# A graph layer and its experts: the 38 lightest nodes as fourth step, the last steps full, scatters bounded and eight gathers later

## The chip, the cores and the metric

The kernel runs on one core of a Trainium2 chip. The metric is the device time of one execution in microseconds (us). The engines are called PE (TensorE), DVE (VectorE), ACT (ScalarE), POOL (GpSimd) and SP (SyncE).

## What is computed

A graph attention layer over 3,750 nodes with 256 features and 123,750 edges, and behind it a mixture of eight experts on every node, both with a residual. Cut to what matters:

```python
feat_all = jnp.einsum('ni,rhid->rnhd', layernorm(x), conv_weights)   # 8 relations, 4 heads of 64
e = leaky_relu(sum(feat_src * attn_l) + sum(feat_dst * attn_r))      # per edge and head
alpha = segment_softmax(e, edge_dst)
x = x + segment_sum(alpha[..., None] * feat_src, edge_dst) + h_bias
xf = layernorm(x)
cw = the two largest of softmax(xf @ gate_w + gate_b), per node
x = x + sum over e of cw[:, e] * (gelu(xf @ W1[e] + b1[e]) @ W2[e] + b2[e])
```

## The kernel before

**Phase 1** (up to about 258 us) works out the row `feat_all` of every (node, relation) and stores it in a table in DRAM, 264 floats a row. Beside it the nodes are ranked by their number of edges (the degree), heaviest first, and each node's row of x goes with its number, the start of its edges, its degree and its norm to `ranked`, where 128 nodes of like degree stand together. 3,750 nodes make 30 groups of 128; the last has only 38 nodes (`LAST`). I call the groups q0 (heaviest) to q29 (the 38 lightest). The other 90 rows of that group are filled from the tile `zeros`.

**Phase 2** works through 30 *windows* w = 0 to 29, one group each (`W` = 30). The line that makes `rank_f` in phase 1 says which group is which window: before, group q goes to window 2q in the first half, and to 57 - 2q in the second, so that heavy and light alternate: q0, q28, q1, q27, ... q14 last but one, and q29, which would be at -1, goes to the end. For a window:

- POOL issues one indirect gather per slot (L907): slot k brings the table row of edge k of each of the 128 nodes. 20 slots always, further ones while k is below the largest degree of the window, up to 40; a window with a larger degree gets its further slots (`xrows`) by 4 or 8 behind the gathers of the next window. A memset behind each second gather (L940) spaces them, and a tiny one (`space_end`, L973) ends a window. `rows` has two buffers, given back in four parts by DVE (`freed`).
- DVE adds the gathered scores (L1043), takes the exponents (with ACT), weighs the rows and adds them up; more than 32 slots take a branch of their own (`weighted(32, 40)` and three adds). I call a window with more than 32 slots heavy, any other light. `post` makes xo (L1173) and its norm z (L1184).
- The experts of window w run on PE (L1497 first product `hid`, L1511 second product `y`) and ACT (gelu, L1389) while DVE and ACT weigh window w + 1; DVE mixes y into xo (L1228, L1236), pair by pair of experts, and writes the row ids `oid` (L1242) to say that xo is ready.
- POOL scatters xo to the output (L915, `scatter`). Inside the gathers of window w it issues the scatter of window w - 3; it waits there for `out_ok`. Its queue is in order, so the gathers behind stand as well. The last three scatters come behind all gathers. DVE's L1173 waits for the scatter of two windows before (`out_done`).

Windows 0 and 1 are written out, the other 28 are a loop of 14 turns with two windows each. Behind the loop come the experts of the last window alone, with `LAST` = 38 nodes: `experts(u, LAST)`, `gelu(u, e, LAST)`, `mix(u, 1, p, st, LAST)`.

Of the kernel before, what the change touches and what calls it, by code (L numbers as in the profile page):

```python
# [20 lines left out]
ALU = mybir.AluOpType  # L21
ACT = mybir.ActivationFunctionType
F32 = mybir.dt.float32
I32 = mybir.dt.int32
# [5 lines left out]
P = 128  # L30
SLOTS = 8
# [133 lines left out]
def phase1(nc, sb, sem, env):  # L165
# [4 lines left out]
    N, D, E, R, H, HD, KD, HC, AGG, ROW, TN, T, J, EJ, W, NF, GN, NBINS, LAST, XW = (env[k] for k in (  # L170
        "N", "D", "E", "R", "H", "HD", "KD", "HC", "AGG", "ROW", "TN", "T", "J", "EJ", "W", "NF", "GN", "NBINS",
        "LAST", "XW"))
# [18 lines left out]
    with ctx:  # L191
# [16 lines left out]
        tmpT = t("tmpT", [TN, T])  # L208
# [29 lines left out]
        rank_f = t("rank_f", [TN, J])  # L238
# [3 lines left out]
        zeros = t("zeros", [P - LAST, XW])  # L242
# [58 lines left out]
        @block.sync  # L301
        def _(sp):
            def load_x(g):
                lo, hi = GROUPS[g]
                for a, b in parts:
                    sp.dma_start(x_all[a:b, lo:hi, 0:D], x_v[a:b, lo:hi, :]).then_inc(x_in[g], 16)

            load_x(0)
            for a, b in parts:
                sp.dma_start(dst_sb[a:b, :], dst_v[a:b, :]).then_inc(dst_in, 16)  # L310
            sp.dma_start(attnb[:, 0, :], attn_l.rearrange("r h d -> (r h d)").partition_broadcast(P)).then_inc(attn_in[0], 16)
            load_x(1)
            sp.dma_start(attnb[:, 1, :], attn_r.rearrange("r h d -> (r h d)").partition_broadcast(P)).then_inc(attn_in[1], 16)
            for a, b in parts:
                sp.dma_start(src_sb[a:b, :], src_v[a:b, :]).then_inc(et_in, 16)
                sp.dma_start(typ_sb[a:b, :], typ_v[a:b, :]).then_inc(et_in, 16)
            load_x(2)
            load_x(3)
            sp.wait_ge(pool_const, 2)
            sp.dma_start(ranked_v[LAST:P, W - 1, :], zeros[:]).then_inc(zero_out, 16)  # L320

            sp.wait_ge(erow_ok, 1)
            for a, b in parts:
                sp.dma_start(edge_row[0:E].rearrange("(p e) -> p e", p=TN)[a:b, :], erow[a:b, :]).then_inc(erow_out, 16)
            sp.dma_start(edge_row[E:GN].rearrange("(p e) -> p e", p=1), zero_u[:]).then_inc(erow_out, 16)

            sp.wait_ge(ranked_out, 16 * J)
            for i, (lo, hi) in enumerate(RANKED):
                sp.dma_start(rank_sb[:, lo:hi, :], ranked_v.bitcast(I32)[:, lo:hi, D:D + 4],
                             allow_slow_non_contiguous=True).then_inc(rank_in[i], 16)  # L330

            for i in range(NSTG):
                sp.wait_ge(stored[i], NP * len(range(i, T, NSTG)))

        @block.gpsimd
        def _(pool):
            g = nc.gpsimd
            g.memset(ident[:], 0.0).then_inc(ident0, 1)
            g.memset(lower[:], 1.0).then_inc(ident0, 1)
            pool.wait_ge(ident0, 2)  # L340
            g.affine_select(out=ident[:], in_=ident[:], compare_op=ALU.not_equal, fill=1.0, base=0,
                            pattern=[[-1, P]], channel_multiplier=1).then_inc(ident_ok, 1)
            g.affine_select(out=lower[:], in_=lower[:], compare_op=ALU.is_ge, fill=0.0, base=-1,
                            pattern=[[1, TN]], channel_multiplier=-1).then_inc(pool_mask, 1)
            g.memset(zero_u[:], 0).then_inc(pool_const, 1)
            g.memset(zeros[:], 0).then_inc(pool_const, 1)
            g.iota(node_i[:], pattern=[[1, J1]], base=0, channel_multiplier=J).then_inc(pool_const, 1)
            g.iota(bin_i[:], pattern=[[1, NBINS]], base=-BIN, channel_multiplier=0).then_inc(pool_const, 1)
            g.iota(slot_i[:], pattern=[[1, CHUNK]], base=0, channel_multiplier=0).then_inc(pool_const, 1)
            for i in range(NSTG):  # L350
                for h in range(H):
                    g.memset(stage[i][:, :, h * HC + HD:h * HC + HD + 1], 1.0).then_inc(cols_ok, 1)

            for j in range(J1):
                if j in (0, JD):
                    pool.wait_ge(chunk_ok, 1 if j == 0 else 2)
                g.indirect_dma_start(dchunk[:, j, :], None, dst.rearrange("(c e) -> c e", e=SEARCH),  # L357
                                     bass.IndirectOffsetOnAxis(chunk_u[:, j:j + 1], 0)
                                     ).then_inc(chunk_in[landing_of(j)], 16)

            pool.wait_ge(rank_ok, 1)
            pool.wait_ge(zero_out, 16)
            for j in range(J):
                g.indirect_dma_start(ranked, bass.IndirectOffsetOnAxis(rank_u[:, j:j + 1], 0), x_all[:, j, :],  # L364
                                     None).then_inc(ranked_out, 16)

            pool.wait_ge(erow_out, NP + 16)
            for w in range(W):
                if w in starts_at:
                    pool.wait_ge(rank_in[starts_at[w]], 16)  # L370
                g.indirect_dma_start(idx_all[:, w, :], None, edge_row.rearrange("(n o) -> n o", o=1),
                                     bass.IndirectOffsetOnAxis(rank_sb[:, w, 1:2].bitcast(U32), 0)
                                     ).then_inc(idx_in, 16)
                g.memset(spacer[:, w, :], 0)
            pool.wait_ge(idx_in, 16 * W)

        @block.vector
        def _(dve):
            v = nc.vector
            st = Steps(dve, dstep)  # L380

            def go(ins):
                st.did(ins)
                st.wait()

            v.memset(ones[:], 1.0).then_inc(ones_ok, 1)
            dve.wait_ge(pool_const, 5)
            st.did(v.tensor_copy(bin_f[:], bin_i[:]))
            st.did(v.tensor_copy(slot_id[:], slot_i[:]))
            go(v.tensor_copy(node_f[:], node_i[:]))  # L390
# [90 lines left out]
            go(v.tensor_scalar(rank_p[:], rank_i[:], P - 1, None, ALU.bitwise_and))  # L481
            go(v.tensor_scalar(rank_i[:], rank_i[:], 7, None, ALU.logical_shift_right))
            go(v.tensor_copy(rank_f[:], rank_i[:]))
            go(v.tensor_scalar(tmpT[:], rank_f[:], -2.0, 2.0 * W - 3.0, ALU.mult, ALU.add))
            go(v.scalar_tensor_tensor(out=rank_f[:], in0=rank_f[:], scalar=2.0, in1=tmpT[:], op0=ALU.mult, op1=ALU.min))
            go(v.tensor_scalar(tmpT[:], rank_f[:], 0.0, float(W), ALU.is_lt, ALU.mult))
            go(v.tensor_tensor(rank_f[:], rank_f[:], tmpT[:], ALU.add))
            v.scalar_tensor_tensor(out=rank_u[:], in0=rank_p[:], scalar=float(W), in1=rank_f[:], op0=ALU.mult,  # L488
                                   op1=ALU.add).then_inc(rank_ok, 1)
# [150 lines left out]
def phase2(nc, sb, sem, env):  # L640
# [258 lines left out]
    def _(pool):  # L899
# [8 lines left out]
                                     bass.IndirectOffsetOnAxis(idx[:, col + k:col + k + 1], 0)  # L908
                                     ).then_inc(landed, 16)

        def scatter(v, par, n=P):

            pool.wait_ge(out_ok, v + 1)
            alone(pool, pool_passed)
            q.indirect_dma_start(out, bass.IndirectOffsetOnAxis(oid[par][0:n, :], 0), xo[par][0:n, :],  # L915
                                 None).then_inc(out_done[par], 16)

        def static_rows(w, par, half):

# [28 lines left out]
            for k in range(SURE):  # L948
                if k == 2 * EDGE and (not isinstance(w, int) or w >= 1):
                    fills(w * 3)  # L950
                if k == SLOTS and (not isinstance(w, int) or w >= 3):
                    scatter(w - 3, 1 - par)
                if k % SLOTS == 0:
                    freed_by(k // SLOTS)
                last = spaced_gather(k)
                if k in (SURE // 2 - 1, SURE - 1):
                    last.then_inc(spaced, 1)
# [48 lines left out]
        windows(pool, window)  # L1006
        scatter(W - 3, 1)
        scatter(W - 2, 0)
        scatter(W - 1, 1, LAST)
        for i in range(2):  # L1010
            pool.wait_ge(out_done[i], 16 * (W // 2))

# [1 line left out]
    def _(dve):  # L1014
# [216 lines left out]
        def mix(u, par, p, st, n=P):  # L1231

            dve.wait_ge(w2_ok, u * NE + 2 * p + 2)
            for e in (2 * p, 2 * p + 1):
                st.wait()
                st.did(v.scalar_tensor_tensor(out=xo[par][0:n], in0=y_ps[p % 2][0:n, (e % 2) * D:(e % 2 + 1) * D],  # L1236
                                              scalar=cw[0:n, e:e + 1], in1=xo[par][0:n], op0=ALU.mult, op1=ALU.add))
# [82 lines left out]
        u = W - 1  # L1320
        st = mix_start(u, 1)
        for p in range(PAIRS):
            mix(u, 1, p, st, LAST)
        finish(u, 1, st)

    @block.scalar
    def _(act):
# [57 lines left out]
        def gelu(u, e, n=P):  # L1385
            act.wait_ge(hid_ok, u * NE + e + 1)
            after(act, w2_ok, u * NE + e - 1)
            for m in range(KH):
                last = a.activation(hT[e % 2][:, m, 0:n], hid_ps[e % 2][:, m * P:m * P + n], ACT.Gelu,  # L1389
                                    bias=b1t[:, e, m:m + 1])  # L1390
            last.then_inc(gelu_ok, 1)
# [63 lines left out]
        z_in(u)  # L1455
        gate_den(u)
        for e in range(NE):
            gelu(u, e, LAST)
            if e == 1:
                cwt_in(u)  # L1460

    @block.tensor
    def _(pe):
# [92 lines left out]
        windows(pe, window)  # L1556
        u = W - 1
        z_turn(u)
        experts(u, LAST)


_INS = ['x', 'src', 'dst', 'edge_type_8', 'L0_gnn_conv_weights', 'L0_gnn_attn_l', 'L0_gnn_attn_r', 'L0_gnn_h_bias',
# [23 lines left out]
```

## Time and profile before

| | |
|---|---|
| median of 3 runs | 1844.96 us (1844.57 to 1847.32) |
| the profiled execution: its time, its span | 1841.54 us, 1839.5 us |
| busy: PE, DVE, ACT, POOL | 1291.8, 1294.8, 778.6, 1334.4 us |
| gathers into `rows`, into `xrows` | 982, 24 |
| first and last gather of window 0 to 29 | 258.21 us to 1737.74 us |
| last scatter starts | 1828.68 us |

Gathers of each window, counted on POOL between its end markers (the degree of the group's heaviest node, at most 40):

| windows | before |
|---|---|
| 0 to 9 | 40, 24, 40, 25, 40, 26, 40, 27, 39, 28 |
| 10 to 19 | 38, 28, 38, 29, 37, 30, 36, 30, 36, 31 |
| 20 to 29 | 35, 31, 35, 32, 34, 32, 34, 33, 33, 21 |

Window 0 has 16 extra slots, windows 2 and 4 have 4 each. Windows 27 and 28 are the groups q15 and q14, window 25 is q16 with 32 slots. The span goes from the first to the last instruction; an engine's busy time says nothing of whether the others wait for it.

### The profile page before, as it was taken

How to read it: one execution, taken by the hardware profiler on the slowest of the kernel's cores; microseconds unless marked ns; L12 is line 12 of the kernel's file. 1: busy time of each engine (PE TensorE's matmuls, PEld its weight loads, DVE VectorE, ACT ScalarE, POOL GpSimd, SP SyncE). 2: the span in 40 equal slices, each digit the busy share in tenths (PEclk: the TensorE clock that was granted, in tenths of full speed). 3: DMA queues.
4: the chain of work that ended last, by engine and by line, in shares of the span. 5: the costliest groups of instructions: out<-in, count | busy, mean ns of one | idle time of the engine just before them, and what ended most of it. 6: DMA issues, size and time to landing. Idle time of an engine off the chain costs nothing.

```text
span 1839.5 us, 28715 instructions
## 1 busy us (share of the span) xinstructions
PE 1291.8 (70%) x6881; PEld 1040.7 (57%) x6881; DVE 1294.8 (70%) x2578; ACT 778.6 (42%) x2829; POOL 1334.4 (73%) x1702
## 2 busy tenths in 40 slices
PE   6999940037684777677767677777777685867787
PEld 2444420026574666666666566667666575756675
DVE  7660032668887888787878787878787878878881
ACT  3544410225354444444444444444444444544441
POOL 0727748688788788888888888888888888888600
PEclk9999975568797888888888888888879797888887
DMA  8758576333333333333333333333333333333300
GB/s 227 228 160 216 162 212 210 82 93 100 83 100 94 89 99 100 101 98 101 99 99 101 100 98 101 98 101 101 100 99 99 98 100 101 99 99 101 81 4 4
DMA packets 86819, 204.06 MB, mean 111 GB/s; under 512 B 32475, under 2 KB 44693, under 8 KB 82371
## 3 DMA queue, kind: packets, MB, share of 16 engines
q0 software_dynamic: 57552, 147.97, 29.8%
q10 hardware_dynamic: 9596, 33.95, 6.1%
q1 hardware_dynamic: 19485, 20.52, 4.0%
q14 instruction: 174, 1.43, 0.3%
q8 instruction: 12, 0.20, 0.0%
HBM read 162.22 MB, written 40.07 MB: 110 GB/s over the span
## 4 chain that ended last, share of the span: by engine, by line
POOL 41%; issue 18%; DVE 12%; PE 5%; DVEq 3%; POOLq 3%; ACT 2%; DMA 1%; ACTq 0%; SPq 0%
POOL rows L907 31%; POOL space_ring L940 7%; DVE fold_ps L1084 3%; PE y_ps L1511 2%; PE hid_ps L1497 2%; DVEq L67 2%; DVE rows L1080 1%; DVE xo L1236 1%; ACT rows L1400 1%; POOL out_dram L915 1%; POOL space_edge L940 1%; POOL xrows L907 1%; POOLq L920 1%; POOLq L964 1%; POOLq L979 1%
## 5 line engine op out<-in xcount | busy, mean ns | idle before, releaser
L907 POOL DMA_INDIRECT rows<-table,idx_st x982 | 943.5, 961 | 253.1 <-issue 243.8
L1511 PE MATMUL y_ps<-w,hT 128*128 128x256 f32 (+1 forms) x1920 | 508.3, 421 | 258.7 <-ACT hT L1389 258.7
L1511 PEld LDWEIGHTS y_ps<-w,hT 128*128 128x128 f32 (+1 forms) x1920 | 385.9, 208 | 345.8 <-ACT hT L1389 282.9
L1497 PE MATMUL hid_ps<-zT,w 128*128 128x128 f32 (+1 forms) x3840 | 497.3, 293 | 0.0
L1497 PEld LDWEIGHTS hid_ps<-zT,w 128*128 128x128 f32 x3840 | 485.9, 208 | 13.3 <-issue 10.8
L1400 ACT ACTIVATE rows<-rows,ex 128x65 f32<-128x65 f32 x1320 | 326.0, 346 | 114.0 <-DVE ex L1071 114.0
L1389 ACT ACTIVATE hT<-hid_ps,b1t 128x128 f32<-128x128 f32 (+1 forms) x960 | 269.6, 363 | 209.9 <-PE hid_ps L1497 208.5
L1084 DVE TENSOR_TENSOR fold_ps<-rows,fold_ps 128x780 f32<-128x780 f32 (+1 forms) x348 | 326.9, 939 | 34.1 <-issue 4.7
L598 PE MATMUL feat_ps<-wc,xnT 128*125 128x512 f32 x480 | 220.7, 604 | 0.5 <-ACT xnT L533 0.5
L1080 DVE TENSOR_TENSOR rows<-rows,fold_ps 128x2340 f32<-128x2340 f32 (+1 forms) x76 | 189.7, 2529 | 3.3 <-issue 3.3
L940 POOL MEMSET space_ring<- 128x400 uint8 x414 | 187.3, 452 | 0.1
L1236 DVE SCALAR_TENSOR_TENSOR xo<-y_ps,cw,xo 128x256 f32<-128x256 f32 (+1 forms) x240 | 115.7, 482 | 37.6 <-PE y_ps L1511 31.3
L598 PEld LDWEIGHTS feat_ps<-wc,xnT 128*125 128x125 f32 x480 | 86.8, 190 | 91.1 <-issue 90.5
L1470 PE MATMUL zt_ps<-ident,z 128*128 128x128 f32 x60 | 16.9, 375 | 154.9 <-DVE z L1184 154.9
L546 ACT COPY stage<-feat_ps 125x512 f32<-125x512 f32 x120 | 69.5, 585 | 115.1 <-PE feat_ps L598 114.9
L915 POOL DMA_INDIRECT out_dram<-xo,oid x30 | 30.2, 1005 | 105.3 <-DVE oid L1242 101.0
L1470 PEld LDWEIGHTS zt_ps<-ident,z 128*128 128x128 f32 x60 | 8.6, 193 | 157.0 <-DVE z L1184 157.0
L1377 ACT COPY zT<-zt_ps 128x256 f32<-128x256 f32 x30 | 11.2, 372 | 180.1 <-PE zt_ps L1470 180.1
L1355 ACT ACTIVATE th<-e_diff 128x160 f32<-128x160 f32 x30 | 10.1, 336 | 173.9 <-DVE e_diff L1061 173.9
L357 POOL DMA_INDIRECT dchunk<-in_dst_dram,chunk_u x31 | 40.5, 1305 | 58.0 <-DVE chunk_u L436 48.8
L1481 PE MATMUL gate_ps<-ident,xnw 128*128 128x128 f32 x60 | 12.0, 284 | 78.7 <-ACT xnw L1366 78.7
L364 POOL DMA_INDIRECT ranked<-x_all,rank_u x30 | 35.7, 1190 | 41.0 <-DVE rank_u L488 32.1
(197 smaller groups left out, 1117.3 us busy)
## 6 DMA issues: line engine op xcount, KB each, us to landing
table<-stage ACTq DMA_DIRECT2D x30, 924.0 KB
rows<-table,idx_st POOLq DMA_INDIRECT x982, 2.8
w<-in_L_ffn_W_dram SPq DMA_DIRECT2D x16, 512.0 KB, 13.8
node_row<-ranked SPq DMA_DIRECT2D x30, 132.0 KB, 2.6
table<-stage ACTq DMA_DIRECT2D x30, 107.2 KB
x_all<-in_x_dram SPq DMA_DIRECT2D x2, 1120.0 KB
wc<-_L_gnn_conv_weights_dram ACTq DMA_DIRECT2D x2, 1024.0 KB, 8.0
attnb<-in_L_gnn_attn_l_dram SPq DMA_DIRECT2D x1, 1024.0 KB, 12.5
```

The lines of the kernel that those rows point to most:

```text
L546: a.copy(stage[i % NSTG][:, b * RB:(b + 1) * RB, 0:AGG].rearrange("p r (h c) -> p r h c", h=H)[:, :, :, 0:HD], feat_ps[b][0:TN, :].rearran ...
L598: last = m.matmul(feat_ps[b][0:TN, :], xnT[i % NXT][:, k, :], wc[:, k, b * BANK:(b + 1) * BANK], start=(k == 0), stop=(k == KD - 1))
L907: q.indirect_dma_start(buf[:, k, :], None, table, bass.IndirectOffsetOnAxis(idx[:, col + k:col + k + 1], 0)).then_inc(landed, 16)
L915: q.indirect_dma_start(out, bass.IndirectOffsetOnAxis(oid[par][0:n, :], 0), xo[par][0:n, :], None).then_inc(out_done[par], 16)
L940: return q.memset(spacing(k // 2), 0)
L1080: return v.tensor_tensor(o, r, bc(ex_ps[:, :, lo:hi].rearrange("p h k -> p k h"), 3, HC), ALU.mult)
L1084: return v.tensor_tensor(lanes[:, 0:n], rows[par][:, lo:lo + n, 0:AGG], lanes[:, 0:n], ALU.add)
L1236: st.did(v.scalar_tensor_tensor(out=xo[par][0:n], in0=y_ps[p % 2][0:n, (e % 2) * D:(e % 2 + 1) * D], scalar=cw[0:n, e:e + 1], in1=xo[par][ ...
L1389: last = a.activation(hT[e % 2][:, m, 0:n], hid_ps[e % 2][:, m * P:m * P + n], ACT.Gelu, bias=b1t[:, e, m:m + 1])
L1400: last = a.activation(r, r, ACT.Copy, scale=ex[:, h, k:k + 1])
L1497: last = t.matmul(hid_ps[e % 2][:, m * P:m * P + n], w1[:, e, k, m * P:(m + 1) * P], zT[:, k, 0:n], start=(k == 0), stop=(k == KD - 1))
L1511: last = t.matmul(y_ps[p % 2][0:n, (e % 2) * D:(e % 2 + 1) * D], hT[e % 2][:, k, 0:n], w2[:, e, k, :], start=(k == 0), stop=(k == KH - 1))
```

## The change

Four things:

1. *The order.* `rank_f` sends group q to window 2q up to q15, and to 61 - 2q from q16 on; q15, which would be at 30, goes to window 1. So the order is q0, q15, q1, q29, q2, q28, q3, q27, ... q14, q16. By the counts above, the gathers are then 40, 33, 40, 21, 40, 24, 40, 25, 39, 26 in windows 0 to 9; 38, 27, 38, 28, 37, 28, 36, 29, 36, 30 in 10 to 19; and 35, 30, 35, 31, 34, 31, 34, 32, 33, 32 in 20 to 29.
2. *The last window is full*: `LAST` goes out of the experts, gelus and mixes behind the loop.
3. *The filling rows* now lie in window 3 and carry the node number 3750 and more; all scatters have a bound, `bounds_check=N - 1`, and rows beyond it are skipped. POOL makes `zeros` with two memsets and an iota in place of one memset.
4. *A scatter's place*: behind gather 16 of a window instead of gather 8.

```diff
-            sp.wait_ge(pool_const, 2)
-            sp.dma_start(ranked_v[LAST:P, W - 1, :], zeros[:]).then_inc(zero_out, 16)
+            sp.wait_ge(pool_const, 4)
+            sp.dma_start(ranked_v[LAST:P, 3, :], zeros[:]).then_inc(zero_out, 16)
...
-            g.memset(zeros[:], 0).then_inc(pool_const, 1)
+            g.memset(zeros[:, 0:D], 0).then_inc(pool_const, 1)
+            g.memset(zeros[:, D + 1:XW], 0).then_inc(pool_const, 1)
+            g.iota(zeros[:].bitcast(I32)[:, D:D + 1], pattern=[[1, 1]], base=N, channel_multiplier=1).then_inc(pool_const, 1)
...
-            dve.wait_ge(pool_const, 5)
+            dve.wait_ge(pool_const, 7)
...
-            go(v.tensor_scalar(tmpT[:], rank_f[:], -2.0, 2.0 * W - 3.0, ALU.mult, ALU.add))
+            go(v.tensor_scalar(tmpT[:], rank_f[:], -2.0, 2.0 * W + 1.0, ALU.mult, ALU.add))
             go(v.scalar_tensor_tensor(out=rank_f[:], in0=rank_f[:], scalar=2.0, in1=tmpT[:], op0=ALU.mult, op1=ALU.min))
-            go(v.tensor_scalar(tmpT[:], rank_f[:], 0.0, float(W), ALU.is_lt, ALU.mult))
+            go(v.tensor_scalar(tmpT[:], rank_f[:], float(W), 1.0 - W, ALU.is_ge, ALU.mult))
...
-        def scatter(v, par, n=P):
+        def scatter(v, par):
 
             pool.wait_ge(out_ok, v + 1)
             alone(pool, pool_passed)
-            q.indirect_dma_start(out, bass.IndirectOffsetOnAxis(oid[par][0:n, :], 0), xo[par][0:n, :],
-                                 None).then_inc(out_done[par], 16)
+            q.indirect_dma_start(out, bass.IndirectOffsetOnAxis(oid[par][:], 0), xo[par][:], None,
+                                 bounds_check=N - 1, oob_is_err=False).then_inc(out_done[par], 16)
...
-                if k == SLOTS and (not isinstance(w, int) or w >= 3):
+                if k == 2 * SLOTS and (not isinstance(w, int) or w >= 3):
                     scatter(w - 3, 1 - par)
...
-        scatter(W - 1, 1, LAST)
+        scatter(W - 1, 1)
...
-            mix(u, 1, p, st, LAST)
+            mix(u, 1, p, st)
...
-            gelu(u, e, LAST)
+            gelu(u, e)
...
-        experts(u, LAST)
+        experts(u)
```

POOL's program inside the loop, at the scatter of window w - 3 within the gathers of window w (`rows<-table` are the gathers, `out_dram<-xo` the scatter). Before:

```order
L907 DMA rows<-table,idx_st 128x264 [waits spaced]
L907 DMA rows<-table,idx_st 128x264
L940 MEMSET space_ring 128x400
L907 DMA rows<-table,idx_st 128x264 x2
L940 MEMSET space_ring 128x400
L915 DMA out_dram<-xo,oid 3750x256 [waits out_ok]
L927 REGISTER_ALU
L907 DMA rows<-table,idx_st 128x264 [waits freed]
```

And now, in the changed kernel, whose lines are numbered two higher here:

```order
L929 REGISTER_ALU
L909 DMA rows<-table,idx_st 128x264 [waits freed]
L909 DMA rows<-table,idx_st 128x264
L942 MEMSET space_ring 128x400
L909 DMA rows<-table,idx_st 128x264 x2
L942 MEMSET space_ring 128x400
L909 DMA rows<-table,idx_st 128x264 x2
L942 MEMSET space_ring 128x400
L909 DMA rows<-table,idx_st 128x264 x2
L942 MEMSET space_ring 128x400
L917 DMA out_dram<-xo,oid 3750x256 [waits out_ok]
L929 REGISTER_ALU
```

The scatter has moved past the eight gathers 8 to 15 and their four memsets, and past one wait for a freed part of the buffer.

The end of ACT's program, the gelus of the last window's experts. Before:

```order
L1377 COPY zT<-zt_ps 128x256
L1381 ACTIVATE gth<-lg,nm 128x8
L1383 ACTIVATE gden<-gth 128x8
L1389 ACTIVATE hT<-hid_ps,b1t 128x38 x8
L1406 COPY cwT<-gate_ps 8x128
L1389 ACTIVATE hT<-hid_ps,b1t 128x38 x24
```

Now:

```order
L1379 COPY zT<-zt_ps 128x256
L1383 ACTIVATE gth<-lg,nm 128x8
L1385 ACTIVATE gden<-gth 128x8
L1391 ACTIVATE hT<-hid_ps,b1t 128x128 x8
L1408 COPY cwT<-gate_ps 8x128
L1391 ACTIVATE hT<-hid_ps,b1t 128x128 x24
```

The instructions and their order are the same; each works on 128 nodes where it worked on 38. The same goes for PE's first products (128x128 in place of 128x38) and DVE's mixes (128x256 in place of 38x256).

## Rows read from the trace of the kernel before

**Rows 1.** Page, part 4: the chain that ended last, by engine.
```profile
POOL 41%; issue 18%; DVE 12%; PE 5%; DVEq 3%; POOLq 3%; ACT 2%; DMA 1%; ACTq 0%; SPq 0%
```

**Rows 2.** Page, part 5: POOL's indirect transfers (count | busy us, mean ns | idle before).
```profile
L907 POOL DMA_INDIRECT rows<-table,idx_st x982 | 943.5, 961 | 253.1 <-issue 243.8
...
L915 POOL DMA_INDIRECT out_dram<-xo,oid x30 | 30.2, 1005 | 105.3 <-DVE oid L1242 101.0
...
L357 POOL DMA_INDIRECT dchunk<-in_dst_dram,chunk_u x31 | 40.5, 1305 | 58.0 <-DVE chunk_u L436 48.8
```

**Rows 3.** Table by stage, line L907: stage, its length, POOL busy (count), clock, DMA.
```profile
654.30:1707.10 1052.80, 692.62 (x726) 0.85 0.37 100
1707.10:1737.90 30.80, 19.96 (x21) 0.78 0.44 97
```

**Rows 4.** POOL in order of time: start, us, engine, line, operation, idle before.
```profile
499.00 1.01 POOL L915 DMA_INDIRECT out_dram<-xo,oid  x1 [6.61 <-DVE oid L1242]
...
607.65 1.01 POOL L915 DMA_INDIRECT out_dram<-xo,oid  x1 [5.55 <-DVE oid L1242]
...
1707.01 0.13 POOL L973 MEMSET space_end<- 128x1 uint8 x1
```

**Rows 5.** DVE in order of time, L1043 of windows 0 to 6, 27 to 29.
```profile
360.04 0.19 DVE L1043 TENSOR_TENSOR score<-score,xrows 128x32 f32<-128x32 f32 x1 [13.63 <-SPq L858]
...
405.27 0.33 DVE L1043 TENSOR_TENSOR score<-score,rows 128x160 f32<-128x160 f32 x1 [0.18 <-issue]
...
448.79 0.38 DVE L1043 TENSOR_TENSOR score<-score,rows 128x160 f32<-128x160 f32 x1 [0.17 <-issue]
...
506.51 0.32 DVE L1043 TENSOR_TENSOR score<-score,rows 128x160 f32<-128x160 f32 x1 [0.26 <-issue]
...
548.05 0.33 DVE L1043 TENSOR_TENSOR score<-score,rows 128x160 f32<-128x160 f32 x1 [0.26 <-issue]
...
590.43 0.19 DVE L1043 TENSOR_TENSOR score<-score,xrows 128x32 f32<-128x32 f32 x1 [5.99 <-SPq L858]
...
615.16 0.32 DVE L1043 TENSOR_TENSOR score<-score,rows 128x160 f32<-128x160 f32 x1 [0.26 <-issue]
...
656.70 0.33 DVE L1043 TENSOR_TENSOR score<-score,rows 128x160 f32<-128x160 f32 x1 [0.26 <-issue]
...
1663.09 0.33 DVE L1043 TENSOR_TENSOR score<-score,rows 128x160 f32<-128x160 f32 x1 [0.26 <-issue]
...
1709.83 0.33 DVE L1043 TENSOR_TENSOR score<-score,rows 128x160 f32<-128x160 f32 x1 [0.26 <-issue]
...
1759.57 0.33 DVE L1043 TENSOR_TENSOR score<-score,rows 128x160 f32<-128x160 f32 x1 [0.26 <-issue]
```

**Rows 6.** Who waited for whom, DVE, 657.1 to 1711: us, times, longest.
```profile
DVE xo L1228 <- issue: 38.0, 11, 3.8
DVE score L1043 <- SPq L858: 29.8, 10, 4.2
...
DVE xo L1236 <- PE y_ps L1511: 10.1, 10, 1.7
```

**Rows 7.** All engines in order of time, end of window 29 and behind it.
```profile
1783.24 3.73 PE L1497 MATMUL hid_ps<-zT,w 128*128 128x128 f32 x32
...
1785.23 1.14 ACT L1389 ACTIVATE hT<-hid_ps,b1t 128x128 f32<-128x128 f32 x4 [4.10 <-PE hid_ps L1497]
1785.47 0.48 DVE L1173 SCALAR_TENSOR_TENSOR xo<-z,valid,xres 128x256 f32<-128x256 f32 x1
...
1789.85 0.41 DVE L1184 TENSOR_SCALAR z<-xo,mv,rstd 128x256 f32<-128x256 f32 x1
...
1802.92 3.76 PE L1497 MATMUL hid_ps<-zT,w 128*128 128x38 f32 x32
...
1804.93 0.84 ACT L1389 ACTIVATE hT<-hid_ps,b1t 128x38 f32<-128x38 f32 x4 [6.49 <-PE hid_ps L1497]
```

**Rows 8.** DVE in order of time, its first use of x.
```profile
10.54 1.08 DVE L397 BATCH_NORM_STATS2 stats<-x_all 125x6 f32<-125x256 f32 x3 [6.91 <-DMA x_all<-in_x_dram]
```

## The prediction

> **What bounds the kernel now.** I read four views. First the chain of work that ended last [rows 1]: GpSimd (POOL) holds 41% of it and nearly all of that is the gather line L907 [rows 2]. Then who waited for whom, and POOL's order in time. In the long stretch from 654.3 to 1707.1 us POOL issues 726 gathers and 22 scatters [rows 3]. With 1.0 us and a 0.3 us gap for a scatter and 0.3 us for the end marker of a window, 22 x 1.6 = 35.2 us are not gathers, so one gather costs (1052.8 - 35.2) / 726 = 1.402 us with its gap and its share of the pacing memsets. POOL waits for nobody there; before it, it waits twice for a scatter whose row ids are late, 6.61 and 5.55 us [rows 4].
>
> Then DVE's row "score + rows" at L1043, the first instruction that needs all of a window's gathered rows; I call its start landed(w) [rows 5]. It reads 405.27 for w=1 and 1709.83 for w=28. In the same long stretch DVE waited for rows 29.8 us in 10 of 22 windows, each time in an even one [rows 6]. So POOL leads by little: one pair of windows takes 2 x 1052.8 / 22 = 95.7 us on POOL, and on DVE (1053.1 - 29.8 + 10 x 0.3) / 11 = 93.3 us. Two more things: an even window carries a pause of 38.0 / 11 = 3.5 us before L1228, where DVE's loop goes back to its start; and the end is not balanced. POOL issues only 21 gathers for the last window (30.8 us, [rows 3]) while DVE needs 49.74 us for window 28, so landed(29) = 1759.57 is set by DVE, some 19 us after the last gather could have landed.
>
> **The change, part by part.** *The order.* The same 30 windows with the same 982 gathers run, so POOL's total stays. What moves is who stands where: 33 gathers instead of 24 in w=1, 21 instead of 25 in w=3, and 32 instead of 21 in w=29. Follow both engines.
>
> w=1: nine more gathers stand ahead of the extra slots of window 0, for which DVE already waits 13.63 us [rows 5]. All of 9 x 1.402 = 12.6 us passes on: landed(1) = 417.9. Window 1 now has over 32 slots, so DVE runs its extra branch. Window 27, heavy and without the loop pause, takes 1709.83 - 1663.09 = 46.7 us; window 1 took 43.5 us light, and four to five us are the branch, so 47.5 us is taken between 46.7 and 48.7: landed(2) = 465.4.
>
> w=2 took 57.7 us and w=3 41.5 us, with no wait for rows: landed(4) = 564.6. w=4 took 67.1 us, of which 5.99 - 0.3 = 5.7 us are a wait for its extra slots [rows 5]. These now come early enough, because POOL has run past DVE: 61.4 us, landed(5) = 626.0. w=5 again 41.5: landed(6) = 667.5, against 656.70 before. So DVE is 10.8 us late there.
>
> POOL in the same stretch: the scatter of w-3 is issued behind gather 16 instead of 8, that is 8 x 1.402 = 11.2 us later. Alone this would swallow the waits of 6.61 and 5.55 us. But DVE is late by then. In the trace the scatter at 499.00 comes 50.2 us after landed(2), the one at 607.65 comes 59.6 us after landed(4), 53.9 us without the 5.7 us wait. So the first now goes out at 465.4 + 50.2 = 515.6, the second at 564.6 + 53.9 = 618.5. POOL is at the second after 1.3 us of scatter, 24 gathers (33.6), window 5 with 24 gathers (35.2), four extra slots (5.0) and 16 gathers (22.4): 613.1. The wait does not vanish, it is still some 5 us. From 618.5: 1.3 for the scatter and 24 gathers at 1.41, so POOL is through window 6 at 653.7, within 1 us of before.
>
> From there to the end of window 28 it has 712 gathers instead of 726: 712 x 1.402 + 35.2 = 1033.4, end 1687.1, and rows land 2.8 us later (1707.01 to 1709.83, [rows 4, 5]): 1689.9. DVE over the same 22 windows: 1053.1 less the waits, 26.8, less 3.1 because w=27 is light now (46.7 against 93.3 - 49.7 = 43.6), 1023.2: landed(28) = 1690.7. Both chains give nearly the same; since whichever is later counts at each window, I take 1691, 18.8 us before 1709.83. Then window 28 unchanged 49.74 and window 29, still light (32 slots), 30.28 us from landed(29) to z [rows 5, 7]. POOL's 32 gathers take 32 x 1.402 + 1.6 = 46.5 us and end at about 1734, landing before DVE comes at 1740.7. This is where the gain lies: the last 11 gathers hide under a DVE window that had covered an idle POOL.
>
> *The scatter's place for those behind it.* Behind it on POOL stand gathers 17 and on. DVE reuses xo two windows later and waits for the scatter. It would go out 22.4 + 1.3 us after a window's gathers end and lands 2.4 us later, some 23.3 us after landed(w); DVE asks for it at L1173, in the light window 29 25.9 us behind landed(29) [rows 5, 7]. It costs nothing; if that cover of 2.6 us were gone (DVE is late, which makes it larger), each us over it would count once per window.
>
> *The last window at full width.* Nothing is narrower any more: 128 columns instead of 38 in the first products and in the gelus. Rows at both widths stand side by side [rows 7]: 32 first-product records 3.76 us at 38 columns, 3.73 at 128; four gelus 0.84 against 1.14. PE goes through a pair of experts in hid then y, and the gelus hide under y except the first of a pair: 4 x 0.30 at most, 0.6 taken. The rule of the Trainium skill speaks against this: "TensorE: Matmul & The Clock Gate", step by step, says that throughput follows the number of moving columns. An estimate by that page: 128 records x 90 columns at 2.4 GHz = 4.8 us, which would make the sum 4.8 us worse. The rows disagree with it here, as the weight loads between the products set their pace.
>
> *The bound in the scatter.* No scatter of the trace has one. Below: nothing. Above: a doubling, 1.0 us each. The nearest rows are POOL's own indirect transfers, 961, 1005 and 1305 ns for three kinds [rows 2]; a spread of 0.34 us. I take 0, since the form alone moves the time by 44 ns between L907 and L915. The 90 skipped rows of w=3 save nothing, they are off the path.
>
> *Start.* Two more small POOL instructions near 2 us, and DVE and SP wait for them; DVE then stands 6.91 us waiting for x anyway [rows 8]. Nothing. The rank formulas have as many instructions as before.
>
> **Sum.** 1709.83 to 1691 is -18.8; +0.6 for the gelus: -18.2 us against the profiled execution's 1841.54 us (span 1839.5 and 2.0 around it), 1823.3. The median shown is 1844.96, 3.4 above that execution, so 1844.96 - 18.2 = 1826.8.
>
> **Rivals.**
> *A, DVE's windows get longer when their pauses go.* In the even windows DVE waited about 3 us, in which PE and ACT caught up with the feed-forward part. L1236 already waits for y_ps 10.1 us in 10 windows [rows 6]. If that becomes the rule, 0.9 us per pair over 11 pairs takes 10 us: 1837. Against it: window 28 began without any wait and took 49.74 us, as the others. 20%.
> *B, the bounded scatter is dear* (the other side). Each us of it counts in POOL's 22 scatters of the long stretch. At the spread of 0.34 us: 7.5 us, 1834. It decides from 18.2 / 22 = 0.83 us each; at a doubling 22 us and 1849, slower. The Trainium skill, "DMA: Bandwidth & Descriptors", SWDGE vs HWDGE, says that GpSimd computes these descriptors in software, so that a test per row would be plain work. For slower 6%, for a loss of part of the gain 6%.
> *C, the order helps nothing*: the late start (10.8 us at landed(6)) is made up only through DVE's 26.8 us of waits. If two thirds of these are no slack, because DVE would have met PE or ACT there instead, 18 us are lost: 1845. 5%, and 2% for worse.
> *D, more gain*: DVE's chain is shorter (w=1 at 46, no wait at 618), and POOL leads: the pair then still costs POOL 94 us, so no more than 5 us: 1822. 8%, of which half below 1821.
>
> **Numbers.** My forecast, 1822 to 1832: 53%. About 0.2%, 3.7 us, is what a measurement of this kernel can tell from no change. Faster by more than that: 53 + 17 (A) + 6 (B) + 8 (D) = 84%; within it: 3 (A) + 5 (C) = 8%; slower 6 + 2 = 8%. The range 1820 to 1839 leaves out most of C, the dear B and the tail of D.
>
> **What would show it.** POOL's gathers of w=1 end near 361 us; landed(1) at 418, landed(2) near 465; scatter waits of a few us in w=4 and w=6 at gather 16; DVE's waits for rows nearly gone up to w=20; landed(28) near 1691, landed(29) near 1741, z near 1771; then 50 us to the end. An L1238 wait that grows in every window shows A; scatters of over 1.3 us show B. I am wrong if landed(28) stays near 1705, or if the last products at 128 columns take over 4 us for 32.

## The result

The changed kernel takes 1820.9 us (median of 4 runs, 1820.09 to 1821.53) against 1846.14 us before (4 runs, 1844.57 to 1848.05): ratio 0.9863, 95% interval 0.9846 to 0.988, 25.2 us less. The forecast was 1826.8 us, 18.2 us less. In a second measurement the pair took 1819.45 and 1842.71 us. The profiled execution takes 1820.09 us with a span of 1818.0, 21.5 us less than the span of before. The profiled execution of before (1841.54 us) lies 4.6 us under the median of its kernel, that of the changed kernel 0.8 us under its own; the other 3.8 us are that.

Part 4 of the page, the chain that ended last, and of part 5 the gathers and scatters of POOL. The lines of the changed kernel are numbered two higher.

```profile
DVE 35%; POOL 14%; issue 11%; PE 11%; DVEq 9%; ACT 5%; POOLq 1%; DMA 0%; ACTq 0%; SPq 0%
...
L909 POOL DMA_INDIRECT rows<-table,idx_st x982 | 944.8, 962 | 247.3 <-issue 236.8
...
L917 POOL DMA_INDIRECT out_dram<-xo,oid x30 | 30.6, 1020 | 82.5 <-DVE oid L1244 78.0
```

Before, POOL held 41% of the chain [rows 1]. Now DVE holds 35% and POOL 14% in this execution. In the repeat of the same kernel, further down, it is the other way round, with 33% for POOL and 20% for DVE. So the two chains are about equally long now, as the forecast had them, and neither leads clearly. The gathers cost what they did, and a bounded scatter 1020 ns for 1005 [rows 2].

POOL in order of time (start, us, engine, line, operation, idle before): the marker behind window 1, the two scatters for which it still waits, the markers behind windows 6 and 28.

```profile
360.41 0.12 POOL L975 MEMSET space_end<- 128x1 uint8 x1
...
515.18 1.03 POOL L917 DMA_INDIRECT out_dram<-xo,oid  x1 [5.61 <-DVE oid L1244]
...
619.71 1.01 POOL L917 DMA_INDIRECT out_dram<-xo,oid  x1 [3.89 <-DVE oid L1244]
...
654.78 0.12 POOL L975 MEMSET space_end<- 128x1 uint8 x1
...
1690.04 0.12 POOL L975 MEMSET space_end<- 128x1 uint8 x1
```

DVE in order of time, landed(w) for w = 1, 2, 4, 5, 6, 28, 29, then z of window 29.

```profile
417.63 0.33 DVE L1045 TENSOR_TENSOR score<-score,rows 128x160 f32<-128x160 f32 x1 [0.18 <-issue]
...
465.17 0.33 DVE L1045 TENSOR_TENSOR score<-score,rows 128x160 f32<-128x160 f32 x1 [0.17 <-issue]
...
566.49 0.32 DVE L1045 TENSOR_TENSOR score<-score,rows 128x160 f32<-128x160 f32 x1 [0.25 <-issue]
...
627.24 0.32 DVE L1045 TENSOR_TENSOR score<-score,rows 128x160 f32<-128x160 f32 x1 [0.26 <-issue]
...
668.82 0.32 DVE L1045 TENSOR_TENSOR score<-score,rows 128x160 f32<-128x160 f32 x1 [0.26 <-issue]
...
1691.97 0.33 DVE L1045 TENSOR_TENSOR score<-score,rows 128x160 f32<-128x160 f32 x1 [0.85 <-SPq L860]
...
1742.17 0.33 DVE L1045 TENSOR_TENSOR score<-score,rows 128x160 f32<-128x160 f32 x1 [0.26 <-issue]
...
1773.17 0.41 DVE L1186 TENSOR_SCALAR z<-xo,mv,rstd 128x256 f32<-128x256 f32 x1
```

| | before | forecast | measured |
|---|---|---|---|
| landed(1) | 405.27 | 417.9 | 417.63 |
| landed(2) | 448.79 | 465.4 | 465.17 |
| scatters that POOL waits for | 499.00, 607.65 | 515.6, 618.5 | 515.18, 619.71 |
| landed(6) | 656.70 | 667.5 | 668.82 |
| POOL behind window 28 | 1707.01 | 1687.1 | 1690.04 |
| landed(28) | 1709.83 | 1691 | 1691.97 |
| landed(29) | 1759.57 | 1740.7 | 1742.17 |
| z of window 29 | 1789.85 | 1771 | 1773.17 |
| z to the last row ids | 37.69 | 38.3 | 33.07 |

Up to z the forecast is within 3 us in every line (the two largest misses are 2.9 us at POOL's marker behind window 28 and 2.2 us at z), and z came 16.7 us earlier than before. The last line is off by 5.2 us, with the sign wrong.

Who waited for whom, DVE, in 660 to 1692 us (us, times, longest), the stretch of [rows 6]:

```profile
DVE xo L1230 <- issue: 38.8, 11, 3.9
...
DVE xo L1238 <- PE y_ps L1513: 12.4, 14, 1.6
DVE score L1045 <- issue: 5.4, 21, 0.3
```

The 29.8 us for rows are gone: in 21 of 23 windows L1045 started after its usual 0.26 us, in the other two it waited 0.65 and 0.85 us. The pause where the loop goes back is what it was, and DVE's waits for y_ps grew only from 10.1 to 12.4 us.

### The profile page after: what moved, and what is told of

Its sections match the earlier page's. It is cut to its first block, busy times and chain, and to the rows that moved or that the text cites. A ratio compares the mean times of both kernels' runs of the same rounds, so it can differ in the third digit from the quotient of the medians.

```text
span 1818.0 us, 28744 instructions
## 1 busy us (share of the span) xinstructions
PE 1287.6 (71%) x6881; PEld 1041.7 (57%) x6881; DVE 1294.0 (71%) x2578; ACT 780.6 (43%) x2829; POOL 1335.7 (73%) x1704
## 3 DMA queue, kind: packets, MB, share of 16 engines
q14 instruction: 174, 1.43, 0.2%
## 4 chain that ended last, share of the span: by engine, by line
DVE 35%; POOL 14%; issue 11%; PE 11%; DVEq 9%; ACT 5%; POOLq 1%; DMA 0%; ACTq 0%; SPq 0%
POOL rows L909 10%; DVE fold_ps L1086 10%; DVEq L67 7%; PE y_ps L1513 5%; PE hid_ps L1499 5%; DVE rows L1082 4%; DVE xo L1238 3%; ACT rows L1402 3%; POOL space_ring L942 2%; DVE er_hot L1040 2%; DVE score L1042 2%; ACT hT L1391 1%; DVE hot L1038 1%; POOL xrows L909 1%; DVE xo L1230 1%
## 5 line engine op out<-in xcount | busy, mean ns | idle before, releaser
L1513 PE MATMUL y_ps<-w,hT 128*128 128x256 f32 x1920 | 512.1, 423 | 235.1 <-ACT hT L1391 235.1
L1513 PEld LDWEIGHTS y_ps<-w,hT 128*128 128x128 f32 x1920 | 393.7, 212 | 318.2 <-ACT hT L1391 259.7
L1499 PE MATMUL hid_ps<-zT,w 128*128 128x128 f32 x3840 | 490.7, 290 | 0.0
L1499 PEld LDWEIGHTS hid_ps<-zT,w 128*128 128x128 f32 x3840 | 479.5, 206 | 12.8 <-issue 10.0
L1391 ACT ACTIVATE hT<-hid_ps,b1t 128x128 f32<-128x128 f32 x960 | 271.9, 365 | 203.6 <-PE hid_ps L1499 203.6
L1238 DVE SCALAR_TENSOR_TENSOR xo<-y_ps,cw,xo 128x256 f32<-128x256 f32 x240 | 115.9, 483 | 38.6 <-PE y_ps L1513 32.3
L917 POOL DMA_INDIRECT out_dram<-xo,oid x30 | 30.6, 1020 | 82.5 <-DVE oid L1244 78.0
L1357 ACT ACTIVATE th<-e_diff 128x160 f32<-128x160 f32 x30 | 10.1, 337 | 150.8 <-DVE e_diff L1063 150.8
```

What stands on the lines that cost most here:

```text
L1499: last = t.matmul(hid_ps[e % 2][:, m * P:m * P + n], w1[:, e, k, m * P:(m + 1) * P], zT[:, k, 0:n], start=(k == 0), stop=(k == KD - 1))
L1513: last = t.matmul(y_ps[p % 2][0:n, (e % 2) * D:(e % 2 + 1) * D], hT[e % 2][:, k, 0:n], w2[:, e, k, :], start=(k == 0), stop=(k == KH - 1))
```

## The experiments

All edits are small; each ran beside the kernel before on its chip. They ran in six sets; in four of them the kernel before took 2336 to 2439 us and not 1843 to 1846, as told at the end under "the pauses". Where that is so the ratio is given as measured, but it decides nothing by itself; what can be read is read within the trace.

### The width of the last window

```diff
-            mix(u, 1, p, st, LAST)
+            mix(u, 1, p, st)
...
-            gelu(u, e, LAST)
+            gelu(u, e)
...
-        experts(u, LAST)
+        experts(u)
```

> The kernel before with one edit: the experts, gelus and mixes behind the loop work on 128 nodes instead of 38 (the scatter still writes 38 rows). My prediction put this at +0.6 us. Theory C (clock): PE keeps the full granted clock behind the loop only when its products are 128 wide, so the stretch from z of window 29 to the last row ids takes 33 us instead of 37.7 and the time falls by about 4.6 us. Theory W (the prediction's): the width is free apart from the gelus, +0.6 us, and the shorter end of the changed kernel is an accident of when the clock rose.

2411.72 us against 2415.69: ratio 0.9983 (0.9956 to 1.001). The table by stage has PE's busy time (instructions), PE's granted clock, and the DMA engines' share. First the kernel before, from z of window 29 to its last row ids, then this kernel:

```profile
1789.80:1801.00 11.20, 10.74 (x53) 0.70 0.04 13
1801.00:1813.00 12.00, 12.00 (x67) 0.86 0.01 1
1813.00:1827.50 14.50, 13.48 (x88) 1.00 0.00 0
```

```profile
2378.10:2388.00 9.90, 9.11 (x59) 1.00 0.04 15
2388.00:2399.00 11.00, 11.00 (x81) 1.00 0.01 1
2399.00:2410.90 11.90, 10.79 (x67) 1.00 0.00 0
```

The narrow end has a granted clock of 0.70 and 0.86 in its first two thirds. Two stretches of it, 10.2 of 37.7 us, are at the lower level, 1.2 GHz:

```profile
1793.10:1799.90 6.80, 6.80 (x28) 0.50 0.05 19
1806.80:1810.10 3.30, 3.30 (x9) 0.50 0.00 0
```

PE's products in order of time at the narrow end of the kernel before, the first, second and fourth group touched by the lower level, the third not:

```profile
1791.69 5.77 PE L1497 MATMUL hid_ps<-zT,w 128*128 128x38 f32 x32
...
1797.60 4.76 PE L1511 MATMUL y_ps<-w,hT 128*38 128x256 f32 x16
...
1802.92 3.76 PE L1497 MATMUL hid_ps<-zT,w 128*128 128x38 f32 x32
...
1806.61 5.33 PE L1511 MATMUL y_ps<-w,hT 128*38 128x256 f32 x16
```

At the upper level the same groups take 3.76 and 3.65 us, so the lower level costs 2.0 + 1.1 + 1.7 = 4.8 us, and 37.7 - 4.8 = 32.9 us would be left. The wide one has 1.00 throughout and takes 32.8 us, though the loop ahead of it was the old one. So the clock is the whole of the difference, and the longer gelus cost next to nothing. The changed kernel reads the same:

```profile
1773.20:1784.00 10.80, 10.34 (x65) 1.00 0.04 14
1784.00:1795.00 11.00, 11.00 (x83) 1.00 0.01 1
1795.00:1806.20 11.20, 10.16 (x63) 1.00 0.00 0
```

A repeat:

> The kernel before with experts, gelus and mixes behind the loop at 128 nodes, nothing else, for a chip on which the kernel before takes about 1845 us. Theory C: z to the last row ids 32.8 to 33.1 us with no half-speed clock, and the time 4.7 us less (ratio 0.9975). Theory W: 37.7 + 0.6 us.

2436.66 against 2439.11 us, 0.9991 (0.9964 to 1.0019). z to the row ids took 32.76 us, no lower clock in it. In all profiles of this study the stretch took 37.7 to 39.0 us with 10.2 us at the lower level in each of the five with 38 columns, and 32.75 to 33.4 us with none in the nine with 128. Both measured ratios lie on the side of a gain, but neither is clear of 1; 4.9 us is 0.2% there. Theory C holds for the stretch, and W falls: in every profile with the narrow end PE lost its clock there, in every one with the wide end it kept it. The edit widens two things at once, the moving side of the first products (128x38 to 128x128) and the loaded side of the second ones (128*38 to 128*128); which of the two matters was not separated.

### The bound alone

```diff
-            q.indirect_dma_start(out, bass.IndirectOffsetOnAxis(oid[par][0:n, :], 0), xo[par][0:n, :],
-                                 None).then_inc(out_done[par], 16)
+            q.indirect_dma_start(out, bass.IndirectOffsetOnAxis(oid[par][0:n, :], 0), xo[par][0:n, :], None,
+                                 bounds_check=N - 1, oob_is_err=False).then_inc(out_done[par], 16)
```

> The kernel before with one edit: every scatter has the bound at the last row; all ids are within it. The prediction took 0 for it, the trace of the changed kernel shows 1020 ns a scatter against 1005. Expected: no change in time, within 1 us, and 1.0 us a scatter. Rival B (the bound is dear): over 1.3 us a scatter, 7 us or more in the time.

2383.51 us against 2415.69, ratio 0.9869 (0.9828 to 0.991). All ids are within the bound, so both programs do the same work, and the only price that the trace shows is 17 ns more a scatter; that this made the kernel 32 us faster is not credible. The number says that, with such pauses, two programs of the same work can differ by more than 1%. What can be read is the price of a scatter, part 5 of the page:

```profile
L907 POOL DMA_INDIRECT rows<-table,idx_st x982 | 937.3, 954 | 346.2 <-issue 251.2
...
L915 POOL DMA_INDIRECT out_dram<-xo,oid x30 | 30.6, 1022 | 564.1 <-DVE oid L1242 529.8
```

1022 ns, 17 more than before. Rival B (over 1.3 us) is out by this price; the times of this set say nothing on it.

### The scatter's place alone, in the old order

```diff
-                if k == SLOTS and (not isinstance(w, int) or w >= 3):
+                if k == 2 * SLOTS and (not isinstance(w, int) or w >= 3):
```

> The kernel before with one edit: a scatter goes out behind gather 16 of a window instead of gather 8; order, widths and scatters otherwise as before. Theory M (two chains, of which the later counts): the two waits of 6.6 and 5.6 us go, POOL ends window 28 12 us earlier (near 1695) and stays the later chain, so landed(28) is near 1698 against 1709.8 and the time is 12 us less, 1834 beside a before of 1846. Rival: the old order is bound by DVE at the end whatever POOL does, then the time moves by less than 3 us. Rival: DVE's L1173 now waits for the later scatter in light windows, then POOL gains and DVE's waits at L1173 grow by 1 us or more in each.

> The kernel before, scatters behind gather 16 and nothing else, for a chip on which the kernel before takes about 1845 us. Theory M as before: both waits of POOL (6.6 and 5.6 us) go, POOL is through window 6 some 12 us earlier and stays the later chain, landed(28) near 1698, time 12 us less (ratio 0.9935). Rival 1: DVE bounds the end of the old order, less than 3 us. Rival 2: DVE waits at L1173 for the later scatter.

> The kernel before, scatters behind gather 16 and nothing else, for a chip on which the kernel before takes about 1845 us. Theory M: both waits of POOL (6.6 and 5.6 us) go, POOL is through window 6 some 12 us earlier and stays the later chain, landed(28) near 1698, time 12 us less (ratio 0.9935). Rival 1: DVE bounds the end of the old order, less than 3 us. Rival 2: DVE waits at L1173 for the later scatter. If the kernel before takes about 2440 us again, POOL's later scatter costs there, as twice before: 1.017 to 1.022.

All three ran with long pauses: 2469.01 against 2415.69 us (ratio 1.0216, 1.0165 to 1.0266), 2478.2 against 2439.11 (1.0166, 1.0131 to 1.0201), 2412.36 against 2336.24 (1.0337, 1.0296 to 1.0379). Who waited for whom on POOL, 700 to 2300 us: first of this kernel (first run), then of the kernel with the bound, whose scatters are at gather 8.

```profile
POOL rows L907 <- DVEq L67: 291.3, 21, 18.8
POOL out_dram L915 <- DVE oid L1242: 208.5, 23, 17.8
```

```profile
POOL out_dram L915 <- DVE oid L1242: 417.6, 24, 35.3
...
POOL rows L907 <- DVEq L67: 71.8, 11, 8.6
```

Where DVE is the later engine, POOL's waiting isn't less, only elsewhere: for freed buffer parts (DVEq) instead of row ids, some 500 us of it in both. Rival 2 did not come: in none of the three does DVE wait more than 0.2 us at L1173. Why the time then is 1.7 to 3.4% longer I did not find. The gain of 12 us that theory M gives this edit where the pauses are short was not measured.

### The new order with the scatter at gather 8

```diff
-                if k == 2 * SLOTS and (not isinstance(w, int) or w >= 3):
+                if k == SLOTS and (not isinstance(w, int) or w >= 3):
```

> The changed kernel with one edit: a scatter goes out behind gather 8 again. Theory M: in windows 4 and 6 POOL stands at gather 8 for row ids that are due at the same time as in the changed kernel (515.2 and 619.7), about 18 and 6 us; 32 gathers instead of 24 stand behind each, so POOL ends window 6 some 11.7 us later, at 666, and is the later chain from there on. landed(28) near 1704, the time 12 us over the changed kernel, 1833. Rival: DVE is the bound of the new order with slack on POOL, then it costs less than 3 us. Rival: DVE is late enough that POOL waits at gather 8 in many later windows too, then it costs over 20 us.

> The changed kernel with scatters behind gather 8 again, for a chip on which the kernel before takes about 1845 us. Theory M as before: POOL stands about 18 and 6 us in windows 4 and 6, is through window 6 near 666 and the later chain from there; landed(28) near 1704, 12 us over the changed kernel (ratio to before 0.994). Rival 1: POOL has slack, less than 3 us over the changed kernel. Rival 2: waits at gather 8 in many windows, over 20 us.

> The changed kernel with scatters behind gather 8 again. On a chip on which the kernel before takes about 1845 us, Theory M: POOL stands about 18 us in window 4 and 6 us in window 6, is through window 6 near 666 and the later chain from there; landed(28) near 1704, 12 us over the changed kernel (1832, ratio to before 0.994). Rival 1: POOL has slack, less than 3 us over the changed kernel. Rival 2: waits at gather 8 in many windows, over 20 us. On a chip with the long pauses: 0.985 to 0.99, as twice before.

Again all with long pauses: 2380.26 against 2415.69 us (ratio 0.9844, 0.9797 to 0.9891), 2406.88 against 2439.11 (0.9882, 0.9851 to 0.9914), 2371.48 against 2416.77 (0.9831, 0.9795 to 0.9867). The kernel was 1.2 to 1.7% faster than the one before in three sets. But this kernel has the bound too, and the bound alone, the same work as before, gave 0.9869 in the first of these sets. So these ratios can't be put down to the order and the full last window. How much of the 25 us is the scatter's, and how much the order's, is open: theory M says 12 us for the scatter, and this wasn't measured.

### The changed kernel again

> The changed kernel itself, beside the kernel before, on the chip of this call. In the first set of experiments the kernel before took 2415 us instead of 1846, with pauses on PE, ACT and DVE in the loop of phase 2 and none in phase 1; there the new order with the scatter at gather 8 took 1.6% less. Theory M holds where the loop has short pauses: ratio near 0.986 if the kernel before takes 1846 again, and the pauses of the first set were that chip's. If the kernel before takes about 2415 us again, the gain is what is left of the scatter's place and the order with pauses of 10 us and more: 0.98 to 1.02, and DVE and POOL wait for each other.

1819.45 us against 1842.71: ratio 0.9873 (0.9853 to 0.9894). So the long pauses belonged to the other sets, not to the kernels. landed(28) is 1688.5, after 2.2 us of waiting for the rows, and from z to the row ids it is 33.2 us. The chain that ended last, part 4 of its page:

```profile
POOL 33%; DVE 20%; issue 15%; PE 7%; DVEq 5%; ACT 3%; POOLq 2%; DMA 0%; ACTq 0%; SPq 0%
```

### The lightest window second

If the two chains are right, another order should do better: the 12.6 us that 33 gathers in window 1 cost at the start can be had back by 21 gathers there. In this order window 1 is q29, the odd windows go on with q28 to q17, q15 is window 27 and q16, light, stays last.

```diff
-            sp.dma_start(ranked_v[LAST:P, 3, :], zeros[:]).then_inc(zero_out, 16)
+            sp.dma_start(ranked_v[LAST:P, 1, :], zeros[:]).then_inc(zero_out, 16)
...
-            go(v.tensor_scalar(tmpT[:], rank_f[:], -2.0, 2.0 * W + 1.0, ALU.mult, ALU.add))
+            go(v.tensor_scalar(tmpT[:], rank_f[:], -2.0, 2.0 * W - 1.0, ALU.mult, ALU.add))
...
-            go(v.tensor_scalar(tmpT[:], rank_f[:], float(W), 1.0 - W, ALU.is_ge, ALU.mult))
+            go(v.tensor_scalar(tmpT[:], rank_f[:], -2.0, 2.0 * W - 4.0, ALU.mult, ALU.add))
+            go(v.scalar_tensor_tensor(out=tmpT[:], in0=rank_f[:], scalar=W - 3.0, in1=tmpT[:], op0=ALU.is_ge, op1=ALU.mult))
```

> The changed kernel with another order: q0, then q29 (the 38 lightest) second, q1, q28, q2, q27 ... q17 in window 25, q15 in 27, q14 in 28, q16 last; filling rows in window 1, one more small DVE instruction in phase 1. Theory M: 21 gathers instead of 33 stand ahead of the extra slots of window 0, so landed(1) is near 401 instead of 418 and window 1 is light; POOL no longer waits in window 4, is through window 6 near 633, and is the later chain to the end with 719 gathers and one more in windows 7 to 28: landed(28) near 1681, 11 us before the changed kernel; window 29 light, so the time is some 10 us under the changed kernel, 1810. Rival: the end is bound by DVE and ACT from window to window whatever stands first, then landed(28) is DVE's 1669 plus what PE adds, and it could be 20 us; or DVE and POOL collide somewhere new and nothing is gained (1820).

> The changed kernel with the order q0, q29, q1, q28, ... q17 in window 25, q15 in 27, q14 in 28, q16 last. On a chip on which the kernel before takes about 1845 us, Theory M: landed(1) near 401, POOL no longer waits in window 4, is through window 6 near 633 and the later chain to the end, landed(28) near 1681, time near 1810 (ratio 0.981 to before, 10 us under the changed kernel). Rival: DVE and ACT bound the end whatever stands first, then up to 20 us under the changed kernel. Rival: a new collision, then 1820 (0.987). On a chip with the long pauses (before 2330 us and more): 0.99 to 1.01, as in the second set.

The first run met long pauses: 2445.09 against 2439.11 us, 1.002 (0.9993 to 1.0046), no gain. The second did not: 1810.95 us against 1843.05, ratio 0.9828 (0.9811 to 0.9845). DVE, landed(w) for w = 1, 28, 29, and POOL's markers behind windows 1, 6 and 28:

```profile
401.92 0.33 DVE L1046 TENSOR_TENSOR score<-score,rows 128x160 f32<-128x160 f32 x1 [0.18 <-issue]
...
1683.14 0.33 DVE L1046 TENSOR_TENSOR score<-score,rows 128x160 f32<-128x160 f32 x1 [0.26 <-issue]
...
1733.34 0.32 DVE L1046 TENSOR_TENSOR score<-score,rows 128x160 f32<-128x160 f32 x1 [0.26 <-issue]
```

```profile
344.05 0.15 POOL L976 MEMSET space_end<- 128x1 uint8 x1
...
634.26 0.13 POOL L976 MEMSET space_end<- 128x1 uint8 x1
...
1680.33 0.12 POOL L976 MEMSET space_end<- 128x1 uint8 x1
```

Expected were 401, 633 and 1681, and 1810 us. Who waited for whom, DVE, 646 to 1684 us:

```profile
DVE xo L1231 <- issue: 40.3, 11, 4.1
DVE score L1046 <- SPq L861: 20.6, 7, 4.1
```

DVE waits for rows again, 20.6 us in 7 windows, the even ones from 14 to 26, and POOL waits for nobody from window 4 on. So POOL is the later chain from window 14 to 26, not from window 6 as expected: rows land 2.8 us after a marker, which is 637.1 for window 6, and DVE came for them only at 645.5. At window 28 the two meet once more (1680.3 + 2.8 = 1683.1). In the chain that ended last POOL holds 45% of this kernel. It is the fastest version of the study. It never ran beside the changed kernel; against the kernel before of its own set it gains 32.1 us, the changed kernel 25.2 and 23.3 us, so it is some 7 to 9 us faster.

## Why the prediction was right, and where its size was off

*The two chains.* Confirmed. DVE was to be late by 12.6 us at landed(1), 16.6 at landed(2) and 10.8 at landed(6); it was late by 12.4, 16.4 and 12.1 us, and by none at window 18 (1228.57 against 1230.84 before), since DVE made it up through its waits for rows. POOL did not end window 28 at 1687.1 but at 1690.0, since it was through window 6 1 us later and its 712 gathers took 1035.3 us and not 1033.4; DVE, arriving for window 28 at the same time, waited 0.85 us for the rows. The two chains met there as worked out. The best support is the other order: worked out by the same two chains before it ran, it came within 1 us at landed(1), 1.3 us at POOL's marker behind window 6, 2.1 at landed(28) and 1 us in the time.

*The scatter's place.* Two waits were forecast to remain, the second of some 5 us; they measured 5.61 and 3.89 us, at 515.18 and 619.71. None came at L1175. What its place is worth alone was not measured with short pauses.

*The window 28 over an idle POOL.* Confirmed: POOL ends the last gathers at 1736.5, DVE comes at 1742.2 and does not wait.

*The last window at full width*, +0.6 us. This is the term that was off, with its sign wrong; it measured -4.6 us (33.07 against 37.69). The prediction compared rows at either width, 3.76 and 3.73 us for 32 first products, and took both from stretches at the upper clock. From 1793.1 to 1799.9 us and from 1806.8 to 1810.1 us the narrow tail ran at the lower one, its first 32 products took 5.77 us and its second ones up to 5.33; this was in the trace of before and I read over it. The experiment with only the width changed shows that it belongs to the width. The measured gain is 7.0 us above the forecast one: 5.2 us are this term, 3.8 come from where the two profiled executions lie among the runs of their kernels, and 2.2 the other way are in z, which came that much later than forecast; 0.2 us is left. That is why 1820.9 us, though inside the range of 1820 to 1839, is 0.9 us from its lower end and under the 1822 to 1832 that I gave the best chance: the mechanism of the order was right, but the number is in the range by little.

*The bound*, 0. Measured 15 to 17 ns a scatter, half a microsecond in all 30.

*Rivals.* A would have shown as growing waits for y_ps; they grew by 2.3 us over 22 windows and not by 10. B and C did not come. D had the time, 1822 and below, but for another reason: it had DVE's window 1 shorter, 46 us, and no wait at the second scatter, and the trace has 47.5 us and 3.89. Neither sign of being wrong came: landed(28) was 1692 and not 1705, and the wide last products took 3.73 to 3.84 us for 32, not over 4. The estimate by the page of the Trainium skill cited for the width was +4.8 us; at the upper level 32 first products take 3.76 us narrow and 3.73 to 3.84 wide, and the whole stretch got 4.6 us shorter, which decides against it here.

## What to carry to other kernels

Where two engines take turns at being late, work out when each could start each step, on both chains, with the counts of every step; the later one counts, and the order of the steps decides where the slack falls. Put the cheap steps where something waits for them to pass (here ahead of the extra slots of window 0), and let the last transfers lie under computation instead of leaving their engine idle there. And do not take from a narrow tail that it is cheap: look at the granted clock of the tail at its present width first.

## What was not expected of the hardware

*The clock and the width.* With the products behind the loop narrowed to 38 nodes PE was busy nearly all the time (36.2 of 37.7 us) and yet was granted 0.70 and then 0.86 of its full clock; with 128 and the same number of instructions (busy 31.5 of 33.0 us), 1.00. "TensorE: Matmul & The Clock Gate" of the Trainium skill, what's actually happening, says that the clock goes by how busy the engine has been; its two levels are seen here, and the busy time of the profile alone does not tell which it will be.

*The pauses.* In four sets, on three chips, the kernel before took 2336 to 2439 us; in the other two sets and in the first measurement it took 1843 to 1846. It is not one speed a chip either: two sets on the same chip have 2415.69 and 2336.24 us for the same kernel before. Phase 1 takes the same, POOL's gathers of window 2 end at 435.9 us with the bound alone, against 437.3 in the profile of before, and a gather takes what it took, 954 ns against 961. In phase 2, ACT, PE and DVE stand still for 10 us and more at a time, for nothing that the profile names. Who waited for whom of the kernel with the bound, ACT in 700 to 2250 us ("remote" is a release for which the profile has no instruction):

```profile
ACT hT L1389 <- remote: 348.6, 57, 15.1
```

The kernel before shows no such row for ACT in 700 to 1700 us. The pauses do not begin with the loop. In eight of the nine profiles that have them ACT stands for 10 to 15 us before a gelu of window 1, which is written out, between 399 and 429 us and with no releaser that the profile names. In the kernel with the bound:

```profile
418.68 1.14 ACT L1389 ACTIVATE hT<-hid_ps,b1t 128x128 f32<-128x128 f32 x4 [14.66 <-remote]
```

There DVE stands 23.3 us at L1228 of window 1, and later 7 to 14 us in both windows of a turn, where the kernel before has 3.5 us once a turn [rows 6]. So it isn't shown that these are the short pause of the loop's return made longer. That it is the fetching of instructions is a guess too; no run tested it, and part 3 of the profile's page shows no more fetching: the larger of the two instruction queues moved 174 packets and 1.43 MB in the kernel before and with the bound alike. What follows is that ratios measured with such pauses (0.987 for an edit that leaves the work as it was) are no measure of a change of 1%.
